# Layer 0 of the first batch item moved into the lanes, and the last bias among the mixtures

## Chip, cores and metric

One core of a Trainium2 chip. The metric is device time in microseconds, the median of several executions: 484.26 us for the kernel before (three executions, 484.23 to 484.34). All data are float32.

## What is computed

x has 32 batch items of 128 channels by 2048 positions. Four conditional residual layers follow each other:

```
x = x + W_a(n) x + b_a(n)                 # layer 0: 128x128 matrix of item n
x = x + conv(x, 9 taps, 4 groups) + ctx(n) + bias      # layer 1
x = x + W_2(n) x + b_2(n)                 # layer 2
x = x + W_3(n) x + b_3(n)                 # layer 3
W_l(n) = sum_k att_l(n, k) * weight_l[k]   # a mixture of 8 matrices
att_l  = softmax(gelu(gelu(cond W0 + b0) W1 + b1) W2 + b2)
```

## The kernel before, in words

The preparation computes the attention shares of all 32 items, the mixtures a0 (layer 0, identity added), a2 and a3, and for each item the product of a2 and a3, called m, so that layers 2 and 3 are one matrix. The biases of the layers are folded into c0 (added behind layer 0), d (behind the convolution) and e (at the end); e is itself a sum of matmuls over a2's bias, a3's weights w3 and a3's own bias.

PSUM has eight banks of 512 columns: four in cv_ps and four in aux_ps. Positions are split into four phases of 512. Three pieces run for each item: layer 0 (`layer0_steps`, L488, into aux_ps), the convolution (`conv_steps`, L508, into cv_ps) and the output product (`out_steps`, L537, into aux_ps). Every operand is split into a high part (fp32r) and a rest (hi and lo), and three matmuls stand for one. Each matmul uses 32 rows of the array; four generators, the lanes (`lane`, L544), one for each quarter of the rows, are advanced in turn by `in_turn` (L561), so that four matmuls on four row groups make a round. A lane starts 2 rounds behind the lane before it (LAG). In rounds, layer 0 and the output product have 12 each and the convolution 36. ScalarE copies each PSUM bank out as the high part (x1_hi, x2_hi), VectorE subtracts it from the bank to get the rest (x1_lo, x2_lo).

Order of PE's work in the preparation (L567 to L589): the hidden layers, the attention transposes with the matmul of bias d between them, 12 rounds of mixtures (`mixtures`, L431, also four row groups in turn; 24 banks in a ring of seven), the small biases, 8 more rounds, bias_e options 0 to 3 (L464, L466; L466 uses all 128 rows), the mixtures' remaining rounds, bias_e options 4 to 7, pair groups 0 to 3 (`quad_product`, L444, four products each, 128 rows, a ring of the four cv_ps banks), layer 0 of item 0 into aux_ps, pair groups 4 to 7, and then the lanes, which begin with layer 0 of item 1. Mixture banks are copied out by ScalarE (L600) and VectorE (L746) in a fixed share; the m banks by ScalarE (L641).

a0 makes a round trip through DRAM, so that each row group gets its own copy: SP saves the first pair, waits, issues four replicas (L286), then loads x of item 1 (L275), saves the other pairs, and so on, in one queue. GpSimd splits a0_rep into a0_hi and a0_lo (L696, L698), for item 0 behind the conversion of the convolution's weights (L722 to L726).

Of the kernel before, what the change touches and what calls it, by code (L numbers as in the profile page):

```python
# [13 lines left out]
B = 32  # L14
L = 2048
K = 8
# [18 lines left out]
DMA = 16  # L35
PAIR = 2
QUAD = 4
REPEAT = 4
HALVES = 2
PER = PH // HALVES  # L40
# [20 lines left out]
def wait(eng, semaphore, value):  # L61

    if value > 0:
        eng.wait_ge(semaphore, value)


def cond_resid_kernel(nc, x, net, consts, mix, bias, conv, c_weight, w3, out):
    with ExitStack() as ctx:
# [184 lines left out]
            return mix_out_a if BY_SCALAR[t] else mix_out_v, sum(by == BY_SCALAR[t] for by in BY_SCALAR[:t + 1])  # L253


        h_ps = [[cv_ps[:, h, 0:REPEAT * B]] + [aux_ps[:, 2 * h + n, 0:REPEAT * B] for n in range(NL - 1)] for h in range(2)]
        logits_ps = cv_ps[:, 2, 0:K]
        att_ps = aux_ps[:, 0, 0:NB].rearrange("p (n b) -> p n b", b=B)
# [8 lines left out]
        def _(sp):  # L267
# [9 lines left out]
            def save(src, scratch, first, last, saved):  # L277

                sp.dma_start(scratch[first:last].rearrange("q p x -> p q x"),
                             src[:, PAIR * first:PAIR * last, :].rearrange("p (q n) m -> p q (n m)",  # L280
                                                                           n=PAIR)).then_inc(saved, DMA)
# [7 lines left out]
            def replicate_a0(pair, phases):  # L289
                if pair < B // PAIR:  # L290
                    sp.wait_ge(a0_saved[min(pair, 1)], DMA)
                    wait(sp, a0_split, 2 * PAIR * (pair - 1))
                    replicate(a0_dram, a0_rep, a0_rep_loaded, pair, phases)
# [31 lines left out]
            load_half(0, 0)  # L325
            load_half(0, 1)
            sp.dma_start(w3_sb, w3.rearrange("p (k m) -> p k m", k=K)).then_inc(e_loaded, DMA)
            sp.dma_start(conv_f[:], conv).then_inc(conv_loaded, DMA)
            sp.wait_ge(d_ready, 1)
            sp.dma_start(d_dram, d_sb[:]).then_inc(d_saved, DMA)  # L330

            sp.wait_ge(*mix_taken(NOG - 2))
            sp.wait_ge(*mix_taken(NOG - 1))
            save(a0_all, a0_dram, 0, 1, a0_saved[0])
            replicate_a0(0, range(PH))
            load(1)
            save(a0_all, a0_dram, 1, B // PAIR, a0_saved[1])
# [33 lines left out]
        def _(pe):  # L371
# [23 lines left out]
            def attention():  # L395


                pe.wait_ge(consts_loaded, DMA)
                pe.wait_ge(shares_ready, 1)
                pe.matmul(att_ps.rearrange("p n b -> p (n b)"), shares[:].rearrange("q c k o -> q (c k o)"),  # L400
                          eye_sb[0:NB, 0:NB], start=True, stop=True).then_inc(att_made, 1)
                bias_d()
                pe.matmul(att_t_ps.rearrange("k n b -> k (n b)"), shares[:, 0, :, 0], eye_sb[0:NB, 0:NB], start=True,
                          stop=True).then_inc(att_t_made, 1)

# [6 lines left out]
            def bias_d():  # L412
                pe.wait_ge(c_weight_loaded, DMA)
                pe.matmul(d_ps, cw_sb[:], cond_sb, start=True, stop=True)
# [41 lines left out]
                          start=True, stop=True)  # L456
                pe.matmul(c2_ps, bias_sb[:, 1, :], att_t[:, 1, :], start=True, stop=True).then_inc(c_made, 1)

            def bias_e(options):
                if 0 in options:  # L460
                    pe.wait_ge(e_loaded, DMA)
                    pe.wait_ge(c2_att_ready, 1)
                    for n in range(1, NL):
                        pe.matmul(e_ps, bias_sb[:, n, :], att_t[:, n, :], start=(n == 1), stop=False)  # L464
                for k in options:
                    mm = pe.matmul(e_ps, w3_sb[:, k, :], c2_att[:, k, :], start=False, stop=(k == K - 1))  # L466
                return mm

            def layer0_steps(n, p):

                if n == 0 and p == 0:

                    pe.wait_ge(e_out, 1)
                pe.wait_ge(a0_split, 2 * (n + 1))

                wait(pe, y_out, PH * (n - 3) + p + 1)
                if n in (1, 2):
                    pe.wait_ge(x1_lo_done, PH * (n - 1) + p + 1)  # L480
                i, steps = 0, 3 * G
                for g in range(G):
                    h = g // PER
                    if g % PER == 0:
                        pe.wait_ge(x_lo_done, HALVES * n + h + 1)
                    hi, lo = x_parts(n, h)
                    for w, a in ((a0_hi, hi), (a0_lo, hi), (a0_hi, lo)):
                        mm = pe.matmul(aux_ps[:, p, :], w[n % 2][rows(p), g, :], a[rows(p), g % PER, :],  # L488
                                       start=(i == 0), stop=(i == steps - 1))
                        i += 1  # L490
                        if i == steps:
                            mm.then_inc(l0_done, 1)
                        yield

            def conv_steps(n, g):

                if n == 0 and g == 0:
                    pe.wait_ge(conv_split, 2)
                    pe.wait_ge(zero_cols, 4)
                    pe.wait_ge(m_out, B // QUAD)  # L500
                if g == 0:
                    pe.wait_ge(x1_lo_done, PH * (n + 1))
                wait(pe, x2_lo_done, PH * (n - 1) + g + 1)
                i, steps = 0, 3 * TAPMATS
                for j in range(TAPMATS):
                    s, q = j // PH, j % PH
                    for w, a in ((conv_hi, x1_hi), (conv_lo, x1_hi), (conv_hi, x1_lo)):
                        mm = pe.matmul(cv_ps[:, g, :], w[rows(g), j, :], a[n % 2][rows(g), q, s:s + T],  # L508
                                       start=(i == 0), stop=(i == steps - 1))
                        i += 1  # L510
                        if i == steps:
                            mm.then_inc(conv_done, 1)
                        yield
# [30 lines left out]
            def lane(g):  # L544

                for _ in range(LAG * g):
                    yield
                for n in range(B - 1):
                    yield from layer0_steps(n + 1, g)
                    conv = conv_steps(n, g)  # L550
                    if 0 < n < B - 2:
                        yield from itertools.islice(conv, CONV_A)
                        yield from out_steps(n - 1, g)
                    yield from conv

                yield from out_steps(B - 3, g)
                yield from conv_steps(B - 1, g)
                yield from out_steps(B - 2, g)
                yield from out_steps(B - 1, g)
# [12 lines left out]
                hidden(1, n)  # L572
            logits()
            fill(8)
            attention()
            mixing = [mixtures(c) for c in range(LANES)]

            in_turn(mixing, 3 * G)
            biases()
            in_turn(mixing, 2 * G)  # L580
            bias_e(range(0, 4))
            in_turn(mixing)
            bias_e(range(4, K)).then_inc(e_made, 1)
            for m in range(4):
                quad_product(m)
            in_turn([layer0_steps(0, p) for p in range(PH)])
            for m in range(4, B // QUAD):
                quad_product(m)
            in_turn([lane(g) for g in range(G)])  # L589

# [1 line left out]
        def _(act):  # L592
# [22 lines left out]
            def x1_out(n, phases=range(PH)):  # L615
                for p in phases:
                    act.wait_ge(l0_done, PH * n + p + 1)
                    nc.scalar.activation(x1_hi[n % 2][:, p, 1:T + 1], aux_ps[:, p, :], ACT.Identity,  # L618
                                         bias=c0_all[:, n:n + 1]).then_inc(x1_hi_done, 1)

            def x2_out(n):
# [22 lines left out]
            for t in range(MIXES):  # L644
                if BY_SCALAR[t]:
                    mix_evacuate(t)
            for m in range(3):
                m_evacuate(m)
            split_second_x_hi(0)
            m_evacuate(3)  # L650
            split_second_x_hi(1)
            act.wait_ge(bias_out, 1)
            x1_out(0)
            for m in range(4, B // QUAD):
                m_evacuate(m)
            for n in range(B):
                if 0 < n:
                    x2_out(n - 1)
# [12 lines left out]
        def _(pool):  # L671
# [47 lines left out]
            for q in range(PH):  # L719

                centre = conv_f[:, PH + q, rows(q)]
                nc.gpsimd.tensor_tensor(centre, centre, eye32_sb, ALU.add).then_inc(pool_chain, 1)  # L722
            pool.wait_ge(pool_chain, PH)
            nc.gpsimd.tensor_copy(conv_hi[:], conv_f[:]).then_inc(conv_split, 1)
            pool.wait_ge(conv_split, 1)
            nc.gpsimd.tensor_tensor(conv_lo[:], conv_f[:], conv_hi[:].bitcast(F32), ALU.subtract).then_inc(conv_split, 1)  # L726
            split_a0(0)
            split_a0(1)
            for n in range(B):
                if n + 2 < B:  # L730
# [4 lines left out]
        def _(dve):  # L735
# [31 lines left out]
            def x1_out(n):  # L767
                for p in range(PH):
                    dve.wait_ge(x1_hi_done, PH * n + p + 1)
                    nc.vector.scalar_tensor_tensor(x1_lo[n % 2][:, p, 1:T + 1], aux_ps[:, p, :], c0_all[:, n:n + 1],  # L770
                                                   x1_hi[n % 2][:, p, 1:T + 1].bitcast(F32), ALU.add,
                                                   ALU.subtract).then_inc(x1_lo_done, 1)

# [140 lines left out]
```

## Time and profile before

| | us |
|---|---|
| median of 3 executions | 484.26 |
| profiled execution | 484.1 |
| its span | 482.3 |
| busy in the span: PE, VectorE, ScalarE, GpSimd | 473.2, 320.2, 248.5, 151.2 |

The span is what the profile sees; the execution's own time has 1.8 us around it. Times of instructions are counted from the span's start. PE matmuls overlap, so the sum of single durations is far above the busy time.

### The profile page before, as it was taken

To read this page: it belongs to the slowest core of one execution; us is meant where nothing else is said; L and a number is where in the kernel's file an instruction comes from. 1 tells how busy PE (TensorE), PEld (TensorE's weight loads), DVE (VectorE), ACT (ScalarE), POOL (GpSimd) and SP (SyncE) were. 2 spreads that over 40 slices of the span, in tenths; PEclk is the share of its full clock that TensorE was granted. 3 is DMA by queue.
4 is the path that set the end of the run, shared out by engine and by line. 5 is a ranking of instruction groups with operands and counts; after the bars stand their busy time and mean duration, and the time that the engine had idled before them with its cause. 6 is when DMAs were issued, how large, how long until landed. Compare 5 with 4: busy or idle time off the path is not lost.

```text
span 482.3 us, 17714 instructions
## 1 busy us (share of the span) xinstructions
PE 473.2 (98%) x8003; PEld 446.3 (93%) x8003; DVE 320.2 (66%) x409; ACT 248.5 (52%) x414; POOL 151.2 (31%) x151
## 2 busy tenths in 40 slices
PE   8989999999999999999999999999999999999996
PEld 7978999999999999999999999999999999999995
DVE  3548687767676876767687776767777676777424
ACT  5654445466544545654455466444545654455544
POOL 2935072324133322414331331333223142420110
PEclk9999999999999999999999999999999999999998
DMA  8696977676546476664746666464667746452224
GB/s 277 207 334 184 302 232 226 209 221 208 186 120 215 156 217 219 207 216 112 211 149 217 209 214 216 129 206 140 215 203 220 220 149 208 131 187 77 90 88 175
DMA packets 39244, 92.86 MB, mean 193 GB/s; under 512 B 4601, under 2 KB 25473, under 8 KB 35201
## 3 DMA queue, kind: packets, MB, share of 16 engines
q1 hardware_dynamic: 39168, 91.73, 60.5%
q8 instruction: 63, 1.03, 0.9%
q14 instruction: 13, 0.10, 0.1%
HBM read 53.95 MB, written 37.77 MB: 190 GB/s over the span
## 4 chain that ended last, share of the span: by engine, by line
PE 97%; DMA 1%; issue 1%; DVE 0%; SPq 0%; DVEq 0%
PE cv_ps L508 59%; PE aux_ps L488 18%; PE aux_ps L537 15%; PE cv_ps L444 2%; PE cv_ps L431 1%; DMA consts_sb<-in_consts_dram 1%; PE cv_ps L537 1%; PE aux_ps L431 1%; PE aux_ps L466 0%; DVE y_all L847 0%; DVE m_all L797 0%; PE aux_ps L455 0%; PE aux_ps L400 0%; SPq L318 0%; SPq L319 0%
## 5 line engine op out<-in xcount | busy, mean ns | idle before, releaser
L508 PE MATMUL cv_ps<-x_hi,conv_lo 32*128 32x512 f32 x1536 | 284.7, 391 | 0.0
L508 PE MATMUL cv_ps<-x_hi,conv_hi 32*128 32x512 f32 x1536 | 284.2, 389 | 0.0
L508 PE MATMUL cv_ps<-x_lo,conv_hi 32*128 32x512 f32 x1536 | 284.2, 391 | 0.0
L508 PEld LDWEIGHTS cv_ps<-x_lo,conv_hi 32*128 32x128 f32 x1536 | 172.5, 184 | 4.7
L508 PEld LDWEIGHTS cv_ps<-x_hi,conv_hi 32*128 32x128 f32 x1536 | 171.5, 183 | 5.6
L508 PEld LDWEIGHTS cv_ps<-x_hi,conv_lo 32*128 32x128 f32 x1536 | 172.4, 183 | 4.5
L779 DVE SCALAR_TENSOR_TENSOR x_lo<-cv_ps,d_all,x_hi 128x512 fp32r<-128x512 f32 x128 | 87.2, 744 | 132.4 <-ACT x_hi L626 132.4
L636 ACT ACTIVATE y_all<-aux_ps,e_all 128x512 f32<-128x512 f32 x122 | 74.0, 689 | 134.1 <-PE aux_ps L537 134.1
L626 ACT ACTIVATE x_hi<-cv_ps,d_all 128x512 fp32r<-128x512 f32 x128 | 77.5, 688 | 67.9 <-PE cv_ps L508 67.9
L488 PE MATMUL aux_ps<-x_hi,a_hi 32*128 32x512 f32 x512 | 99.5, 391 | 2.3 <-issue 2.3
L488 PE MATMUL aux_ps<-x_hi,a_lo 32*128 32x512 f32 x512 | 99.1, 388 | 0.0
L488 PE MATMUL aux_ps<-x_lo,a_hi 32*128 32x512 f32 x512 | 99.0, 388 | 0.0
L537 PE MATMUL aux_ps<-x_hi,m_hi 32*128 32x512 f32 x496 | 94.8, 387 | 0.0
L537 PE MATMUL aux_ps<-x_hi,m_lo 32*128 32x512 f32 x496 | 94.3, 387 | 0.0
L753 DVE TENSOR_TENSOR x_lo<-x_sb,x_hi 128x1024 fp32r<-128x1024 f32 x62 | 86.8, 1401 | 10.3 <-ACT x_hi L612 8.2
L537 PE MATMUL aux_ps<-x_lo,m_hi 32*128 32x512 f32 x496 | 93.5, 384 | 0.0
L770 DVE SCALAR_TENSOR_TENSOR x_lo<-aux_ps,c_all,x_hi 128x512 fp32r<-128x512 f32 x128 | 87.3, 745 | 1.6
L696 POOL CAST a_hi<-a_rep 128x512 fp32r<-128x512 f32 x32 | 26.6, 830 | 189.2 <-DMA a_rep<-a_pairs 124.7
L618 ACT ACTIVATE x_hi<-aux_ps,c_all 128x512 fp32r<-128x512 f32 x128 | 77.5, 691 | 12.9 <-PE aux_ps L488 12.9
L488 PEld LDWEIGHTS aux_ps<-x_hi,a_hi 32*128 32x128 f32 x512 | 58.8, 183 | 4.5 <-issue 2.4
L488 PEld LDWEIGHTS aux_ps<-x_lo,a_hi 32*128 32x128 f32 x512 | 58.5, 183 | 2.1
L488 PEld LDWEIGHTS aux_ps<-x_hi,a_lo 32*128 32x128 f32 x512 | 58.6, 184 | 1.7
(104 smaller groups left out, 455.5 us busy)
## 6 DMA issues: line engine op xcount, KB each, us to landing
x_sb<-in_x_dram SPq DMA_DIRECT2D x31, 1024.0 KB, 6.5
out_dram<-y_all SPq DMA_DIRECT2D x60, 512.0 KB, 7.4
a_rep<-a_pairs SPq DMA_DIRECT2D x64, 128.0 KB, 7.3
m_rep<-m_pairs SPq DMA_DIRECT2D x64, 128.0 KB, 6.1
out_dram<-y_all SPq DMA_DIRECT2D x8, 256.0 KB, 2.6
a_pairs<-a_all SPq DMA_DIRECT2D x1, 1920.0 KB, 12.4
m_pairs<-m_all SPq DMA_DIRECT2D x1, 1792.0 KB, 12.2
m_all<-in_mix_dram SPq DMA_DIRECT2D x2, 512.0 KB, 5.5
```

The costliest lines, as they stand in the source:

```text
L431: mm = pe.matmul(mix_ps[t % MIX_RING][:, P * j:P * (j + 1)], mix_f[layer][rows(c), G * h + j, :], spread[rows(c), layer].rearrange("p b o ...
L444: mm = pe.matmul(prep_ps[m % RING][:, P * k:P * (k + 1)], a23_all[0][:, n, :], a23_all[1][:, n, :], start=True, stop=True)
L488: mm = pe.matmul(aux_ps[:, p, :], w[n % 2][rows(p), g, :], a[rows(p), g % PER, :], start=(i == 0), stop=(i == steps - 1))
L508: mm = pe.matmul(cv_ps[:, g, :], w[rows(g), j, :], a[n % 2][rows(g), q, s:s + T], start=(i == 0), stop=(i == steps - 1))
L537: mm = pe.matmul(out_bank(n, p), w[n % 2][rows(p), g, :], a[n % 2][rows(p), g, :], start=(i == 0), stop=(i == steps - 1))
L618: nc.scalar.activation(x1_hi[n % 2][:, p, 1:T + 1], aux_ps[:, p, :], ACT.Identity, bias=c0_all[:, n:n + 1]).then_inc(x1_hi_done, 1)
L626: nc.scalar.activation(x2_hi[n % 2][:, g, :], cv_ps[:, g, :], ACT.Identity, bias=d_all[:, g, n:n + 1]).then_inc(x2_hi_done, 1)
L636: nc.scalar.activation(y_all[:, k % YBUFS, p % PER, :], bank[:, p, :], ACT.Identity, bias=e_all[:, n:n + 1]).then_inc(y_out, 1)
L696: nc.gpsimd.tensor_copy(a0_hi[n % 2][:], src).then_inc(a0_split, 1)
L753: nc.vector.tensor_tensor(lo, x_sb[n % 2][:, PER * h:PER * (h + 1)], hi.bitcast(F32), ALU.subtract).then_inc(x_lo_done, 1)
L770: nc.vector.scalar_tensor_tensor(x1_lo[n % 2][:, p, 1:T + 1], aux_ps[:, p, :], c0_all[:, n:n + 1], x1_hi[n % 2][:, p, 1:T + 1].bitcast(F32 ...
L779: nc.vector.scalar_tensor_tensor(x2_lo[n % 2][:, g, :], cv_ps[:, g, :], d_all[:, g, n:n + 1], x2_hi[n % 2][:, g, :].bitcast(F32), ALU.add, ...
```

## The change

Five edits. (1) `bias_d` is issued ahead of `attention`, so ahead of its wait for the shares. (2) `bias_e` becomes a generator that is advanced with the mixtures: behind the small biases it lets four rounds pass and then issues one step a round, two of L464 and eight of L466. (3) All eight pair groups are issued in one row behind the mixtures. (4) Layer 0 of item 0 is the first piece of the lanes and writes into the banks of cv_ps (`l0_bank`); phase p waits until the pair group that last used its bank is copied out. The wait for e_out moves to item 1, and ScalarE copies all eight groups ahead of item 0's x1, with the two halves of item 1's x_hi behind groups 3 and 5. (5) The DMA that loads the convolution's weights is issued behind the save of the first a0 pair, and GpSimd splits item 0's a0 ahead of converting these weights.

```diff
+        def l0_bank(n, p):
+            return prep_ps[p] if n == 0 else aux_ps[:, p, :]
...
-            sp.dma_start(conv_f[:], conv).then_inc(conv_loaded, DMA)
             sp.wait_ge(d_ready, 1)
...
             save(a0_all, a0_dram, 0, 1, a0_saved[0])
+            sp.dma_start(conv_f[:], conv).then_inc(conv_loaded, DMA)
             replicate_a0(0, range(PH))
...
-                bias_d()
...
+            def bias_e():
+                for _ in range(E_BEHIND):
+                    yield
+                pe.wait_ge(e_loaded, DMA)
+                pe.wait_ge(c2_att_ready, 1)
+                for n in range(1, NL):
+                    pe.matmul(e_ps, bias_sb[:, n, :], att_t[:, n, :], start=(n == 1), stop=False)
+                    yield
+                for k in range(K):
                     mm = pe.matmul(e_ps, w3_sb[:, k, :], c2_att[:, k, :], start=False, stop=(k == K - 1))
+                    if k == K - 1:
+                        mm.then_inc(e_made, 1)
+                    yield
...
             def layer0_steps(n, p):
-                if n == 0 and p == 0:
-                    pe.wait_ge(e_out, 1)
                 pe.wait_ge(a0_split, 2 * (n + 1))
-                wait(pe, y_out, PH * (n - 3) + p + 1)
-                if n in (1, 2):
-                    pe.wait_ge(x1_lo_done, PH * (n - 1) + p + 1)
+                if n == 0:
+                    pe.wait_ge(m_out, RING + p + 1)
+                elif n == 1:
+                    if p == 0:
+                        pe.wait_ge(e_out, 1)
+                elif n == 2:
+                    pe.wait_ge(x1_lo_done, PH + p + 1)
+                else:
+                    pe.wait_ge(y_out, PH * (n - 3) + p + 1)
...
+                yield from layer0_steps(0, g)
                 for n in range(B - 1):
...
             fill(8)
+            bias_d()
             attention()
...
-            in_turn(mixing, 2 * G)
-            bias_e(range(0, 4))
-            in_turn(mixing)
-            bias_e(range(4, K)).then_inc(e_made, 1)
-            for m in range(4):
-                quad_product(m)
-            in_turn([layer0_steps(0, p) for p in range(PH)])
-            for m in range(4, B // QUAD):
+            in_turn([*mixing, bias_e()])
+            for m in range(B // QUAD):
                 quad_product(m)
...
-            for m in range(3):
+            for m in range(B // QUAD):
                 m_evacuate(m)
-            split_second_x_hi(0)
-            m_evacuate(3)
-            split_second_x_hi(1)
+                if m in (3, 5):
+                    split_second_x_hi(m // 5)
             act.wait_ge(bias_out, 1)
             x1_out(0)
-            for m in range(4, B // QUAD):
-                m_evacuate(m)
...
+            split_a0(0)
             pool.wait_ge(pool_chain, PH)
...
-            split_a0(0)
             split_a0(1)
```

## Rows read from the trace of the kernel before

**Rows 1.** Page, PE's busy time, share of the span, instructions

```profile
PE 473.2 (98%) x8003; PEld 446.3 (93%) x8003; DVE 320.2 (66%) x409; ACT 248.5 (52%) x414; POOL 151.2 (31%) x151
```

**Rows 2.** Chain that ended last: start us, us, what

```profile
19.23 1.01 PE aux_ps L466 x8
20.26 3.84 PE cv_ps L444 x32
24.10 2.26 issue
26.36 3.48 PE aux_ps L488 x44
29.84 3.77 PE cv_ps L444 x32
...
62.79 3.28 PE cv_ps L508 x54
...
76.72 3.27 PE cv_ps L508 x55
```

**Rows 3.** Timeline of GpSimd: start us, us, instruction, count, idle before

```profile
18.48 0.83 POOL L722 TENSOR_TENSOR conv_f<-conv_f,consts_sb 128x32 f32<-128x32 f32 x4
19.38 1.46 POOL L724 CAST conv_hi<-conv_f 128x1536 fp32r<-128x1536 f32 x1
...
24.30 0.61 POOL L696 CAST a_hi<-a_rep 128x512 fp32r<-128x512 f32 x1
24.99 1.26 POOL L698 TENSOR_TENSOR a_lo<-a_rep,a_hi 128x512 fp32r<-128x512 f32 x1
```

**Rows 4.** Timeline of PE: bias d, first matmuls of the lanes

```profile
8.71 0.33 PE L414 MATMUL aux_ps<-m_rep,cw_sb 128*128 128x32 f32 x2
...
33.54 0.51 PE L488 MATMUL aux_ps<-x_hi,a_hi 32*128 32x512 f32 x2
```

**Rows 5.** Timeline of ScalarE

```profile
18.14 1.08 ACT L600 ACTIVATE m_all<-aux_ps 128x512 f32<-128x512 f32 x2 [1.52 <-PE aux_ps L431]
19.11 1.09 ACT L600 ACTIVATE m_all<-cv_ps 128x512 f32<-128x512 f32 x2
...
27.35 1.06 ACT L612 ACTIVATE x_hi<-x_sb 128x1024 fp32r<-128x1024 f32 x1 [3.51 <-DMA x_sb<-in_x_dram]
...
36.59 2.42 ACT L618 ACTIVATE x_hi<-aux_ps,c_all 128x512 fp32r<-128x512 f32 x4 [2.34 <-PE aux_ps L488]
45.02 2.42 ACT L626 ACTIVATE x_hi<-cv_ps,d_all 128x512 fp32r<-128x512 f32 x4 [6.00 <-PE cv_ps L508]
```

**Rows 6.** Timeline of VectorE

```profile
19.26 0.69 DVE L746 COPY m_all<-cv_ps 128x512 f32<-128x512 f32 x1 [0.19 <-PE cv_ps L431]
...
45.81 2.73 DVE L779 SCALAR_TENSOR_TENSOR x_lo<-cv_ps,d_all,x_hi 128x512 fp32r<-128x512 f32 x4 [0.86 <-ACT x_hi L626]
```

**Rows 7.** Timeline of SP's queue: start and length of the issue

```profile
17.90 2.61 SPq L286 DMA_DIRECT2D a_rep<-a_pairs  x4
20.56 0.44 SPq L275 DMA_DIRECT2D x_sb<-in_x_dram  x1
```

**Rows 8.** Page, DMA issues: count, KB, us from issue to landing

```profile
a_pairs<-a_all SPq DMA_DIRECT2D x1, 128.0 KB, 4.4
```

**Rows 9.** Timeline of PE where mixtures and the last bias meet

```profile
14.60 0.34 PE L431 MATMUL cv_ps<-spread,a_rep 32*128 32x128 f32 x1
...
15.12 0.36 PE L431 MATMUL cv_ps<-spread,a_rep 32*128 32x128 f32 x2
...
15.81 0.38 PE L464 MATMUL aux_ps<-att_t,bias_sb 8*128 8x32 f32 x2
16.12 1.08 PE L466 MATMUL aux_ps<-c_att,m_rep 128*128 128x32 f32 x8
17.13 0.37 PE L431 MATMUL aux_ps<-spread,a_rep 32*128 32x128 f32 x1
...
17.35 0.27 PE L431 MATMUL cv_ps<-spread,a_rep 32*128 32x128 f32 x1
```

More of the change, by code:

```diff
@@ L37 @@
 QUAD = 4
+E_BEHIND = 4
 REPEAT = 4
@@ L457, in biases @@
                 pe.matmul(c2_ps, bias_sb[:, 1, :], att_t[:, 1, :], start=True, stop=True).then_inc(c_made, 1)
[L459 to L465, printed above, removed]
+            def bias_e():
[7 more added lines that the diff above has]
+                for k in range(K):
                     mm = pe.matmul(e_ps, w3_sb[:, k, :], c2_att[:, k, :], start=False, stop=(k == K - 1))
-                return mm
+                    if k == K - 1:
+                        mm.then_inc(e_made, 1)
+                    yield
             def layer0_steps(n, p):
-                if n == 0 and p == 0:
-                    pe.wait_ge(e_out, 1)
                 pe.wait_ge(a0_split, 2 * (n + 1))
-                wait(pe, y_out, PH * (n - 3) + p + 1)
-                if n in (1, 2):
-                    pe.wait_ge(x1_lo_done, PH * (n - 1) + p + 1)
+                if n == 0:
[7 more added lines that the diff above has]
+                    pe.wait_ge(y_out, PH * (n - 3) + p + 1)
                 i, steps = 0, 3 * G
@@ L487, in layer0_steps @@
                     for w, a in ((a0_hi, hi), (a0_lo, hi), (a0_hi, lo)):
-                        mm = pe.matmul(aux_ps[:, p, :], w[n % 2][rows(p), g, :], a[rows(p), g % PER, :],
+                        mm = pe.matmul(l0_bank(n, p), w[n % 2][rows(p), g, :], a[rows(p), g % PER, :],
                                        start=(i == 0), stop=(i == steps - 1))
@@ L499, in conv_steps @@
                     pe.wait_ge(zero_cols, 4)
-                    pe.wait_ge(m_out, B // QUAD)
                 if g == 0:
@@ L617, in x1_out @@
                     act.wait_ge(l0_done, PH * n + p + 1)
-                    nc.scalar.activation(x1_hi[n % 2][:, p, 1:T + 1], aux_ps[:, p, :], ACT.Identity,
+                    nc.scalar.activation(x1_hi[n % 2][:, p, 1:T + 1], l0_bank(n, p), ACT.Identity,
                                          bias=c0_all[:, n:n + 1]).then_inc(x1_hi_done, 1)
@@ L769, in x1_out @@
                     dve.wait_ge(x1_hi_done, PH * n + p + 1)
-                    nc.vector.scalar_tensor_tensor(x1_lo[n % 2][:, p, 1:T + 1], aux_ps[:, p, :], c0_all[:, n:n + 1],
+                    nc.vector.scalar_tensor_tensor(x1_lo[n % 2][:, p, 1:T + 1], l0_bank(n, p), c0_all[:, n:n + 1],
                                                    x1_hi[n % 2][:, p, 1:T + 1].bitcast(F32), ALU.add,
```

## The prediction

> **What bounds the kernel now.** I began with the page's first lines: PE is busy 98% of the span [rows 1]. Then the chain of waits in order of time [rows 2]: nearly all of it is PE, and in steady state an item repeats every 76.72 - 62.79 = 13.93 us. An item is 12 + 36 + 12 = 60 rounds of four row-tiled matmuls, so a round is 0.232 us. The chain names PE through the lanes without a break; the change leaves every one of those rounds in place, so it can act only ahead of and at the start of the lanes. There the chain has one hole, 2.26 us at 24.10, between the fourth pair group and layer 0 of item 0. The GpSimd timeline says what it is [rows 3]: a0_hi and a0_lo of item 0 come behind the conversions of conv and end at 26.25; PE resumes at 26.36.
>
> **What goes.** Before, from the first pair group (20.26) to the first lane matmul (33.54, [rows 2, 4]) 13.28 us pass: 3.84 for four groups, the 2.26, 3.41 for layer 0 of item 0 with its own slow start and end, 3.77 for the other four groups. After, the eight groups stand in one row, 3.84 + 3.77 = 7.61 us, and layer 0 of item 0 is 12 more rounds of the lanes, 12 x 0.232 = 2.79. The lag of six rounds is paid once in either kernel. 13.28 - 10.40 = 2.88 us go, if nothing is late.
>
> **What is late next.** Measure from S, the end of the pair groups.
> - The first convolution. Lane 0 reaches it 24 rounds after S, S + 5.57, and waits for x1_lo of all four phases. Lane 0's layer 0 is through at S + 2.79; ScalarE starts on such a bank 0.26 after it (36.59 against 33.54 + 2.79) [rows 4, 5]; VectorE starts 0.79 after ScalarE (45.81 against 45.02) and takes 2.73 for four [rows 5, 6]. Sum S + 6.57: a new wait of 1.0 us. Before, item 0's x1 was made while PE ran groups 4 to 7, so nothing waited. Bounds: 0.7, if four x1_lo took only their pitch behind the last ScalarE one, and 1.3. I take 1.0.
> - The a0 splits. GpSimd now takes item 0's a0 ahead of the conversions of conv. From the arrival R of a0_rep: 1.95 for item 0, 5.0 for conv_hi and conv_lo, 1.95 for item 1, R + 9.0 [rows 3]. Layer 0 of item 1 wants it at S + 2.79. R is at most about 22.3 (the four replicas were issued at 17.90 to 20.51, [rows 7], and had arrived when GpSimd came to them at 24.30), which gives 31.3: in time for S above 28.5. The conv parts are wanted later still.
> - Groups 4 to 7 on ScalarE. It does m 0 to 3, x_hi(1,0), m 4, 5, x_hi(1,1), m 6, 7. Item 1's x landed at 27.35 [rows 5], issued at 20.56 behind the a0 round trip, whose save took 4.4 us [rows 7, 8]. With conv out of the queue ahead of that save it may come back up to 2 us sooner: arrival X between 25.4 and 27.4. From X, two splits of 0.96 and four copies of 0.55 each end at X + 4.2, and phase 3 wants the last of them at S + 1.4. That costs nothing if S is above X + 2.8, and up to 1.9 if S stays near 27.9 and X at 27.35.
>
> **The last bias among the mixtures.** This decides the sign. Before, its two shares stand in blocks: eight L466 matmuls in 1.08 us, a pitch of 0.11, twice [rows 9, 2]; the second block, from 19.23, hides the evacuation of the last mixture banks (ScalarE until 20.20, VectorE until 19.95 [rows 5, 6]), and the first group starts at 20.26. After, one step (two passes) of it stands in each of rounds 16 to 25 of the mixtures. The first two (L464, 8 rows) are row-tiled like the mixtures and cost about their pitch. The eight of L466 use all 128 rows. What the trace shows of going between the two: the last L464 starts at 16.19 - 0.27 = 15.92 and the first L466 at 16.12, 0.20 later; the last L466 starts at 17.20 - 0.28 = 16.92 and the first mixture matmul at 17.13, 0.21 later; that round's second pass then comes at 17.35, 0.22 later instead of 0.09 to 0.11 (15.12, two in 0.36) [rows 9]. So a mixture round with one L466 step in it is 0.21 + 0.02 (four lanes' starts) + 0.20 + 0.13 (the step's second pass, a little over the pitch of the block) + 0.21 = 0.77 us, where the mixture round is 0.22 (two passes) and the bias step in a block 0.22. Rounds 16 and 17 start at 14.60 [rows 9], less 0.14, because the d bias now stands ahead of the wait for the shares instead of between two matmuls behind it (two passes in 0.33, of which mixtures can win some 0.14; 0 to 0.26 [rows 4]). 14.46 + 2 x 0.45 = 15.36, + 8 x 0.77 = 21.52, + the last round's second pass and latency 0.21 + 0.27 = 22.0. Then nothing covers the last evacuation: 0.03 + 0.69 + 0.05 [rows 6]. The first group starts at 22.8, 2.5 later than before. Evacuation (one bank of 0.6 to 0.7 a round of 0.77, on two engines) does not bind there.
> Lower bound: switches overlap fully, a round with its step costs 0.22 + 0.22 = 0.44; 15.36 + 3.6 + 0.5 + 0.8 = 20.2, no change. Upper bound: another 0.1 for each of 16 switches, 24.4. I take 22.8, since it is made of the gaps that these very two kinds of matmul show.
>
> The page "TensorEngine Tiling (Array Packing)", section Key Properties, of the Trainium skill says that changing the tiling mode drains TensorE; the gaps of 0.20 and 0.21 agree, as no L466 starts until the tile matmuls before it are about over. Its page "TensorE: Matmul & The Clock Gate", section "Step-by-step: what each phase is for", says that weight loads are pulled ahead of running matmuls where row groups don't conflict or the spare weight buffer takes them. By that second rule alone the round would come to 0.44 and the sum to the lower bound; it stands as the first rival.
>
> **The sum.** -2.88 + 1.0 + 2.5 = +0.65 us; S is then 30.4, so neither the a0 splits (31.3 against 33.2) nor ScalarE (X + 2.8 at most 30.2) is late. Moving conv's load costs nothing by itself: it is issued about 13.9, behind the save, into a queue that before had passed all loads and the save by 17.90 [rows 7, 8]; GpSimd came to conv_f only at 18.48 [rows 3], and the converted weights are wanted at S + 6.6. The profiled execution took 484.1 (span 482.3 and 1.8 around it); the median is 484.26. 484.1 + 0.65 = 484.75, beside the median 484.9; I say 484.8. About 0.2% (0.97 us) is what a measurement of this kernel can tell from no change.
>
> **Rivals.**
> 1. Interleaved steps are nearly free (0.44 a round). First group at 20.2, S = 27.8. Then X counts: with X = 25.6 ScalarE is late by 0.4. -2.88 + 1.0 + 0.4 = -1.5: 482.7. For it: behind the first L466 block ScalarE waited 1.52 us on PE [rows 5], a wait that spreading the steps removes. Against it: the gaps. Chance 0.17.
> 2. Half of it: switches cost, but the slow second pass overlaps, and some of the steps fall into waits for banks. 0.6 a round, first group at 21.4. -2.88 + 1.0 + 1.2 = -0.7: 483.5. Chance 0.25.
> 3. On the other side: the a0 round trip gets late. The 768 KB of conv now go into the one queue between the save of the first a0 pair and its replicas. If the replicas come 3.5 us late, R is near 26, a0 of item 1 is ready at 35 against S + 2.79 = 33.2, and item 1's x is late by as much (X = 30, ScalarE 34.2 against 31.8). The larger of the two, 2.4 us, comes on top: +3.0, 487.2. It decides from R = 24.2 or X = 27.6. Against it: before, conv stood ahead of the save as well, and both were in by 17.90 [rows 7]. Chance 0.08.
> 4. The change doesn't do what it says, as the hole moves: the new wait is over 1.3 us, and each switch costs 0.05 more than its gap (0.8 in all, half of the upper bound's extra). -2.88 + 1.3 + 3.3 = +1.7: 485.9. Chance 0.12.
> My forecast (within 0.8 of +0.65) has 0.38.
>
> **The numbers.** Faster by over 0.2%: nearly all of rival 1, a third of rival 2: 0.24. Slower by over 0.2%: rivals 3 and 4 and a fifth of the forecast: 0.27. Within: 0.49. The range goes from rival 1 to rival 4, 482.6 to 486.0; the forecast's own is 484.0 to 485.6.
>
> **What would show it.** In PE's timeline L466 matmuls in pairs, 0.77 apart, from about 15.8 to 21.3; the first L444 at 22.8 (20.2 for rival 1); eight groups without a hole, 7.6 us; at once L488 into the convolution's banks; a gap of 1.0 ahead of the first L508, released by VectorE's x1_lo; no gap after it, and 13.93 us for each item. GpSimd's a0 before conv_hi. The forecast is wrong if the first group starts before 21.5, if a gap appears between groups or inside layer 0 of item 0, or if a later item is longer.

## The result, and the profile after

The changed kernel takes 489.85 us (median of 4 executions, 489.09 to 492.64) against 484.30 (median of 4, 484.23 to 485.70): ratio 1.0123, 95% interval 1.0092 to 1.0154. I had said 484.8 and at most 486.0. It is slower by 5.5 us, well outside the range. In this document an execution that is over 1.5% above the fastest of its kernel, at a lower clock, is left out of ratios, intervals and ranges of times.

The profiled execution took 490.46, its span is 488.7 (before: 482.3). Its chain of waits in order of time (start us, us, what), beside [rows 2]:

```profile
18.21 0.34 PE aux_ps L473 x2
...
18.98 0.34 PE aux_ps L473 x2
...
19.75 0.34 PE aux_ps L473 x2
...
20.61 0.57 PE aux_ps L473 x2
...
21.92 0.56 PE aux_ps L473 x2
...
23.22 0.56 PE aux_ps L473 x2
...
24.51 0.56 PE aux_ps L473 x2
...
26.67 9.23 PE cv_ps L448 x64
35.91 3.00 PE cv_ps L500 x36
...
38.98 0.70 ACT x_hi L625
...
39.78 1.72 DVE x_lo L774 x3
...
41.77 0.75 DVE x_lo L774
...
42.66 0.47 PE cv_ps L519
```

L473 is the old L466, L448 the pair groups, L500 layer 0, L519 the convolution. The first bias steps stand 0.77 us apart (18.21, 18.98, 19.75), as forecast; but from the fifth on they stand 1.30 apart, and the pair groups take 9.23 us instead of 7.61. The stretches of the profile after say why (length, busy time and count of PE, PE's weight loads, VectorE, ScalarE, GpSimd, then the granted TensorE clock, DMA share, GB/s):

```profile
10.00:15.00 5.00, 5.00 (x96) 4.94 (x97) 3.21 (x7) 2.88 (x5) 4.34 (x5) 0.66 0.63 243
20.00:25.00 5.00, 5.00 (x35) 3.85 (x34) 0.69 (x1) 2.05 (x4) 1.87 (x6) 0.53 0.94 248
25.00:30.00 5.00, 4.12 (x18) 3.85 (x18) 0.79 (x2) 0.74 (x2) 4.92 (x3) 0.50 1.07 387
30.00:35.00 5.00, 5.00 (x45) 5.00 (x44) 1.06 (x1) 3.83 (x7) 2.60 (x3) 0.94 0.89 314
```

The granted clock is at 0.5, its lower level of 1.2 GHz, from 20.3 to 30.6 us, and once before that, from 10.1 to 13.5. In the profile of before it stands at 1.00 in every such stretch from 5 to 40 us. PE counts as busy in these rounds (5.00 of 5.00 from 20 to 25 us), so how little it does in these rounds is read off the starts of its matmuls and off their count, 35 in 5 us.

GpSimd (timeline), beside [rows 3]: item 0's a0 now comes first, but a0_rep is there only at 23.89, and item 1's a0 is ready at 32.68.

```profile
20.91 0.83 POOL L726 TENSOR_TENSOR conv_f<-conv_f,consts_sb 128x32 f32<-128x32 f32 x4 [2.10 <-DMA conv_f<-in_conv_dram]
23.89 0.61 POOL L700 CAST a_hi<-a_rep 128x512 fp32r<-128x512 f32 x1 [2.15 <-DMA a_rep<-a_pairs]
24.57 1.26 POOL L702 TENSOR_TENSOR a_lo<-a_rep,a_hi 128x512 fp32r<-128x512 f32 x1
...
27.33 3.46 POOL L731 TENSOR_TENSOR conv_lo<-conv_f,conv_hi 128x1536 fp32r<-128x1536 f32 x1
30.71 0.62 POOL L700 CAST a_hi<-a_rep 128x512 fp32r<-128x512 f32 x1
31.41 1.27 POOL L702 TENSOR_TENSOR a_lo<-a_rep,a_hi 128x512 fp32r<-128x512 f32 x1
```

**Where the 6.4 us of the two spans are.** The first pair group starts 6.41 later (26.67 against 20.26 [rows 2]). Of that 1.5 are there at the small biases already (L454 started at 12.55, its successor at 14.03: the clock of 10.1 to 13.5, and a start 0.3 us later). Another 2.2 are what the lower clock costs from the fifth bias step on: the steps start 0.86, 1.31, 1.30 and 1.29 after each other, and the round behind the last one takes 1.30 (24.51 to 25.81), all five instead of 0.77. The 2.7 that remain are the price of the steps and of the last evacuation at the upper clock; the forecast has them at 2.7 as well, less 0.14 for the first edit. The groups cost 1.6 more. Then -2.88, and +1.2 for the wait ahead of the first convolution. 6.41 + 1.6 - 2.88 + 1.2 = 6.3, which is how much later the first convolution starts (42.66 against 36.39). From that convolution to PE's end it is 441.9 us, against 441.5 before: the lanes are nearly what they were. The executions at 489.1 and 489.2 have a mean granted clock of 0.989 against 0.985 in the profiled one, as they would without the first fall; but the one at 492.64 has 0.988, and none of them has a trace, so this isn't shown.

### The profile page after: what moved, and what is told of

The parts are those of the page before. It is cut to its first block, busy times and chain, and to the rows that moved or that the text cites. A ratio compares the mean times of both kernels' runs of the same rounds, so it can differ in the third digit from the quotient of the medians.

```text
span 488.7 us, 17713 instructions
## 1 busy us (share of the span) xinstructions
PE 480.3 (98%) x8003; PEld 421.5 (86%) x8003; DVE 320.0 (65%) x409; ACT 249.4 (51%) x414; POOL 153.9 (31%) x151
## 4 chain that ended last, share of the span: by engine, by line
PE 97%; DVE 1%; ACT 1%; DMA 0%; issue 0%; DVEq 0%; ACTq 0%
PE cv_ps L519 55%; PE aux_ps L548 18%; PE aux_ps L500 16%; PE cv_ps L448 2%; PE cv_ps L435 2%; PE cv_ps L548 1%; PE aux_ps L435 1%; PE aux_ps L473 1%; PE cv_ps L500 1%; DVE x_lo L774 1%; DMA m_rep<-in_net_dram 0%; PE aux_ps L390 0%; ACT L613 0%; PE cv_ps L390 0%; DVE y_all L851 0%
## 5 line engine op out<-in xcount | busy, mean ns | idle before, releaser
L519 PE MATMUL cv_ps<-x_hi,conv_hi 32*128 32x512 f32 x1536 | 326.2, 389 | 1.1 <-DVE x_lo L774 1.1
L519 PE MATMUL cv_ps<-x_hi,conv_lo 32*128 32x512 f32 x1536 | 326.6, 391 | 0.0
L519 PE MATMUL cv_ps<-x_lo,conv_hi 32*128 32x512 f32 x1536 | 326.3, 391 | 0.0
L519 PEld LDWEIGHTS cv_ps<-x_hi,conv_hi 32*128 32x128 f32 x1536 | 236.5, 183 | 13.4 <-issue 1.4
L519 PEld LDWEIGHTS cv_ps<-x_lo,conv_hi 32*128 32x128 f32 x1536 | 236.8, 184 | 13.0
L519 PEld LDWEIGHTS cv_ps<-x_hi,conv_lo 32*128 32x128 f32 x1536 | 236.7, 183 | 11.1
L500 PE MATMUL aux_ps<-x_lo,a_hi 32*128 32x512 f32 x496 | 115.4, 388 | 0.0
L500 PE MATMUL aux_ps<-x_hi,a_lo 32*128 32x512 f32 x496 | 115.1, 388 | 0.0
L500 PE MATMUL aux_ps<-x_hi,a_hi 32*128 32x512 f32 x496 | 114.9, 389 | 0.0
L757 DVE TENSOR_TENSOR x_lo<-x_sb,x_hi 128x1024 fp32r<-128x1024 f32 x62 | 84.4, 1362 | 10.1 <-ACT x_hi L619 8.0
L548 PEld LDWEIGHTS aux_ps<-x_hi,m_hi 32*128 32x128 f32 x496 | 81.4, 183 | 3.2
L548 PEld LDWEIGHTS aux_ps<-x_hi,m_lo 32*128 32x128 f32 x496 | 81.6, 183 | 2.6
L548 PEld LDWEIGHTS aux_ps<-x_lo,m_hi 32*128 32x128 f32 x496 | 81.7, 183 | 2.5
L500 PEld LDWEIGHTS aux_ps<-x_hi,a_lo 32*128 32x128 f32 x496 | 80.7, 184 | 3.1
```

What stands on the lines that cost most here:

```text
L500: mm = pe.matmul(l0_bank(n, p), w[n % 2][rows(p), g, :], a[rows(p), g % PER, :], start=(i == 0), stop=(i == steps - 1))
L548: mm = pe.matmul(out_bank(n, p), w[n % 2][rows(p), g, :], a[n % 2][rows(p), g, :], start=(i == 0), stop=(i == steps - 1))
L757: nc.vector.tensor_tensor(lo, x_sb[n % 2][:, PER * h:PER * (h + 1)], hi.bitcast(F32), ALU.subtract).then_inc(x_lo_done, 1)
```

## The experiments

Each is timed beside the kernel before, which had a median of 484.2 to 484.3 in all calls.

**1. Which part costs: four kernels.** The bias back in two blocks, all else as changed:

```diff
-            in_turn([*mixing, bias_e()])
+            in_turn(mixing, 2 * G)
+            last_bias = bias_e()
+            in_turn([last_bias], NL - 1 + 4)
+            in_turn(mixing)
+            in_turn([last_bias])
```

> The changed kernel with one edit undone: the last bias stands in two blocks again, as before the change. Theory A (the interleaved 128-row steps cost 0.77 us a round, and their gaps bring TensorE's clock down to the lower level until the pair groups are over): the first pair group starts near 20.2 us, the clock stays at its upper level from there, the span loses the 2.88 us and pays about 1.2 for the wait ahead of the first convolution: 482.5 to 483.0 us. Theory B (eight pair groups in a row, or layer 0 in the lanes, bring the clock down, wherever the bias stands): the groups still take 9.2 us or more, 485 to 487 us.

Measured: 486.74 us, 1.0039 (1.0025 to 1.0053). The groups take 7.41, so theory B is out; but it isn't 482.5 to 483.0 either. Its chain of waits has left PE:

```profile
23.92 0.62 POOL a_hi L704
...
24.61 1.27 POOL a_lo L706
25.88 1.42 POOL conv_hi L733
...
27.37 3.46 POOL conv_lo L735
30.82 1.56 POOL a_hi L704
...
32.46 2.14 POOL a_lo L706
...
34.64 0.64 PE aux_ps L500
```

Layer 0 of item 1 waits 1.89 us for its a0, ready at 34.6, and right behind that hole the clock is at its lower level from 34.8 to 38.2. The changed kernel hid this, since its groups end at 35.9. Splitting item 1's a0 took 3.8 us here instead of 1.9, while VectorE was splitting item 1's x out of SBUF:

```profile
27.82 5.64 DVE L761 TENSOR_TENSOR x_lo<-x_sb,x_hi 128x1024 fp32r<-128x1024 f32 x2 [5.26 <-ACT x_hi L623]
```

That slowdown is the whole hole: with 1.95 for the split, a0 would have been ready at 30.78 + 1.95 = 32.73 (an estimate), and PE was through with item 0 at 32.75. Part of the rest of the miss is the clock at the start, which rose only at 14.4 in this profile.

The bias step alone, on the kernel before (`bias_e` made a generator as in the change):

```diff
-            in_turn(mixing, 2 * G)
-            bias_e(range(0, 4))
-            in_turn(mixing)
-            bias_e(range(4, K)).then_inc(e_made, 1)
+            in_turn([*mixing, bias_e()])
```

> The kernel before with only the last bias interleaved with the mixtures. Theory A: the first pair group starts 22.7 to 26, the hole ahead of layer 0 of item 0 closes (a0 is ready at 26.25), and the clock falls during the interleaved rounds as in the changed kernel: 487 to 489 us, nearly the whole loss. Theory B: the drain alone, +2.5 less the hole of 2.26: 484.5 to 485 us, clock at its upper level.

Measured: 489.17 us, 1.0097 (1.0077 to 1.0116). One edit has nearly the whole loss; the first group starts at 25.10, and the clock is low from 18.8 to 29.0, again from the fifth bias step on (19.04).

The fifth edit alone, on the kernel before:

```diff
-            sp.dma_start(conv_f[:], conv).then_inc(conv_loaded, DMA)
...
             save(a0_all, a0_dram, 0, 1, a0_saved[0])
+            sp.dma_start(conv_f[:], conv).then_inc(conv_loaded, DMA)
...
+            split_a0(0)
             pool.wait_ge(pool_chain, PH)
...
-            split_a0(0)
             split_a0(1)
```

> The kernel before with only the fifth edit: conv's load behind the save of the first a0 pair, and item 0's a0 split ahead of conv's conversions. Both theories: a0 of item 0 is ready near 24.3 instead of 26.25 and the hole of 2.26 us shrinks to 0.2 to 0.5; 482.3 to 482.8 us. If the replicas come later behind conv's 768 KB (rival 3 of the prediction) the hole stays: 484 us.

Measured: 485.14 us, 1.0014 (1.0004 to 1.0023): a small loss, not a gain. The hole ahead of item 0 did shrink, to 0.19 us at 24.14; a new one of 1.48 us opened at 31.55 ahead of item 1, whose a0 came behind conv's conversions, and again the clock was low for 3.4 us behind it (34.1 to 37.5). I had looked at the first hole only.

```profile
33.03 0.70 PE L488 MATMUL aux_ps<-x_hi,a_hi 32*128 32x512 f32 x2 [1.49 <-POOL a_lo L698]
```

The split of this a0 took 3.8 us here too (29.16 to 32.98), beside VectorE's split of x; with 1.95 it would have been ready at 31.1 (an estimate), ahead of the 31.54 at which PE wanted it.

The eight L466 steps cut to 8 rows, which leaves most of the last bias's sum out; nothing else is changed:

```diff
-   mm = pe.matmul(e_ps, w3_sb[:, k, :], c2_att[:, k, :], start=False, stop=(k == K - 1))
+   mm = pe.matmul(e_ps, w3_sb[0:K, k, :], c2_att[0:K, k, :], start=False, stop=(k == K - 1))
```

> The changed kernel with the eight L466 steps cut to 8 rows, so that they are row-tiled like the mixtures (this leaves most of the last bias's sum out). Same number of instructions in the same places. Theory A (it is the change of tiling and its gaps): rounds of 0.35 to 0.45 us instead of 0.77, the first group near 20.3, clock at the upper level: 482.5 to 483.3 us. Rival (it is the number of instructions among the mixtures, or their semaphores): rounds stay near 0.77 and the time stays at 489 us.

Measured: 486.34 us, 1.0032 (1.0018 to 1.0046). The steps stand 0.45 us apart, with the same number of instructions, and the clock stays up among them:

```profile
20.65 0.03 PE aux_ps L473
...
21.09 0.03 PE aux_ps L473
...
21.54 0.03 PE aux_ps L473
```

So the price of a round is that of going from row-tiled to 128-row matmuls and back. The forecast of 482.5 to 483.3 was missed all the same. In the profile the clock is low from 9.4 to 19.6, just ahead of these steps, and PE waits 1.07 us for the last mixture banks, which ScalarE copies until 24.05; the first group starts at 24.10, not near 20.3. Item 1's a0 is ready at 34.0 there, just ahead of its use at about 34.3; that an execution with an earlier start has to wait for it isn't shown.

**2. Why the clock falls, and what a switch costs.** Three matmuls on zeros behind each step (they take one bank out of the mixtures' ring, which has six then instead of seven):

```diff
                     mm = pe.matmul(e_ps, w3_sb[:, k, :], c2_att[:, k, :], start=False, stop=(k == K - 1))
+                    for _ in range(FILLERS):
+                        pe.matmul(aux_ps[:, 0, 0:2 * P], idle_sb[:, 0:P], idle_sb[:], start=True, stop=True)
```

> The changed kernel with three matmuls of 256 columns on zeros behind each L466 step (24 in all, into a PSUM bank taken out of the mixtures' ring, which has six banks instead of seven). Theory A (TensorE's clock falls because the interleaved rounds leave it idle between the switches): with more work in each gap-ridden round the clock stays at its upper level; a round costs 0.77 + 0.35, the first group starts near 25.7, the groups take 7.6 again: 487 to 488 us, less than the 489.85 of the changed kernel although there is more to do. Rival (the clock falls at that point whatever PE does): the fillers cost twice as much, 491 to 493 us.

Measured: 492.14 us, 1.0134 (1.0108 to 1.0160). The time falls in the rival's range and above my 487 to 488, the trace goes against the rival: the clock never falls among the bias steps or the groups. The fillers (L476) come every 1.20 to 1.21 us from the first round to the last, where the changed kernel went from 0.77 to 1.30:

```profile
20.03 0.44 PE aux_ps L476 x3
21.24 0.43 PE aux_ps L476 x3
...
26.06 0.43 PE aux_ps L476 x3
27.26 0.43 PE aux_ps L476 x3
28.46 0.43 PE aux_ps L476 x3
```

The stretches have the granted clock at 1.00, where the changed kernel had 0.53 and 0.50:

```profile
20.00:25.00 5.00, 5.00 (x55) 3.98 (x55) 1.58 (x3) 1.19 (x2) 1.36 (x5) 1.00 0.94 264
25.00:30.00 5.00, 4.30 (x38) 3.21 (x36) 0.94 (x3) 1.79 (x3) 4.84 (x4) 1.00 1.01 353
```

The mean granted clock is 0.999 in the three executions that count, against 0.985 to 0.989 for the changed kernel. The fillers cost 0.43 a round, not 0.35, and the clock rose only at 14.9 in the profile, so the first group starts at 30.18 instead of 25.7; what the smaller ring adds to that was not tested. So with more work in the rounds the clock holds, whatever the time since the start; but bought with idle work it isn't worth its price.

Two bias steps a round in four rounds, on the kernel before with the bias interleaved (marked against the kernel of one step a round):

```diff
-                    yield
+                    if k % 2:
+                        yield
```

> The kernel before with the last bias among the mixtures, but two L466 steps a round in four rounds: 8 switches of tiling instead of 16, the same matmuls. Theory A (each switch has a price): four rounds of 0.99 and the rest of 0.22, first group near 21.3 if the clock holds: 484.3 to 485.5 us against 489.17 with one step a round; PE's share is higher in such a round, so the clock should hold longer. Rival (the price is in the interleaving as such): 488 to 489 us.

Measured: 487.15 us, 1.0058 (1.0032 to 1.0083), between the kernel before and the one with one step a round, above my 484.3 to 485.5, and wide: 483.9 to 490.1. In the profiled one (492.61) the clock was low from 9.2 to 33.1, so its rounds can't be held against 0.99; but at that same low clock a round with two steps took 1.73 us (22.302 to 24.035) where the changed kernel's round with one took 1.30. The second step adds 0.43 and the way there and back is paid once. Five of the other eleven executions kept a mean granted clock of 0.993 or more, which none of the fifteen did that the three kernels with one step a round have between them (the changed one, the bias step alone, and the one interleaved again in part 3: 0.985 to 0.991). With half the switches the clock falls for less time, in some executions.

**3. The other edits.** The third and fourth alone, on the kernel before (the parts of the change's diff in `layer0_steps`, `lane`, the row of groups and ScalarE's order):

> The kernel before with only the third and fourth edit: all pair groups in one row, layer 0 of item 0 first in the lanes, in the convolution's banks. Item 1's x then comes at 27.35 as before. Theory: -2.88, +1.2 for the wait ahead of the first convolution, and ScalarE's last m copy at 27.35 + 4.2 = 31.5 against 29.3, +2.2: 484.8 us, with PE's holes inside layer 0 of item 0. Rival (the order of the groups pays on its own): 482.5 to 483 us.

Measured: 484.47 us, 1.0009 (0.9995 to 1.0024). The number is right; the mechanism was not seen. In the profile the clock was low from 9.0 to 19.3, so the groups ended at 31.3 and ScalarE was in time. Whether holes inside layer 0 of item 0 stand behind the faster executions (483.6 and up) stays open.

Then a version without both losses: bias in blocks, conv's load put behind item 1's x, both first a0 splits ahead of conv:

```diff
             save(a0_all, a0_dram, 0, 1, a0_saved[0])
-            sp.dma_start(conv_f[:], conv).then_inc(conv_loaded, DMA)
             replicate_a0(0, range(PH))
             load(1)
+            sp.dma_start(conv_f[:], conv).then_inc(conv_loaded, DMA)
...
+            split_a0(0)
+            split_a0(1)
             pool.wait_ge(conv_loaded, DMA)
...
-            split_a0(0)
...
-            split_a0(1)
```

> The changed kernel with the bias in two blocks, conv's load put behind item 1's x, and GpSimd converting conv behind both first a0 splits. Theory C (in the kernel with the blocks the time is lost where a0 of item 1 waits for conv's conversions on GpSimd, ready at 34.6): a0 of item 1 is ready by 24 to 26 us, no wait ahead of layer 0 of item 1, only 1.2 us ahead of the first convolution, no fall of the clock there: 482.3 to 482.9 us. Rival (the lanes' start itself is slow): as with the blocks, 485 to 487 us.

Measured: 483.28 us, 0.9982 (0.9962 to 1.0001), not to be told from the kernel before and above my 482.3 to 482.9. Both first a0 are ready by 26.8. No hole but the 1.04 us ahead of the first convolution. The executions spread from 481.9 to 484.4, with two at 486: in the profiled one the clock rose only at 14.1.

The same kernel with the bias interleaved again:

> The best kernel so far (bias in blocks, conv's load behind item 1's x, both first a0 splits ahead of conv's conversions: 483.28 us) with one edit: the last bias interleaved again, one step a round. Theory A (drains 2.5 us, and the clock falls in these rounds until the groups are over, 3 to 4 us more): 487 to 490 us, clock at the lower level from about 19 or 20 us on, rounds of 0.77 turning to 1.29. Rival (in the changed kernel it was the late a0 of item 1 behind conv that cost most, and the interleaving only 2.5): 485 to 486 us.

Measured: 489.28 us, 1.0106 (1.0089 to 1.0123). With no late a0 the one edit costs 6 us, with the clock low from 20.4 to 30.6, here from behind the sixth step:

```profile
19.26 0.34 PE aux_ps L473 x2
...
20.03 0.34 PE aux_ps L473 x2
...
21.10 0.56 PE aux_ps L473 x2
...
22.39 0.56 PE aux_ps L473 x2
...
24.55 10.26 PE cv_ps L448 x64
34.81 2.99 PE cv_ps L500 x39
```

More filling at the start (`fill(12)` for `fill(8)`), and bias d between the transposes again:

> The best kernel so far with 12 instead of 8 filling matmuls ahead of the attention. Theory D (the spread of its runs, 481.9 to 486.6, is the clock at the start: it falls again near 9 to 10 us or rises only at 14, and nothing downstream absorbs that shift any more): a denser start makes the late rise or the fall rarer, median 482.3 to 482.8, though 0.2 to 0.9 us are lost where the clock is low while it fills. Rival (these matmuls don't decide it): same median, 483.3, same spread.

> The best kernel so far with the first edit undone: the matmul of bias d between the two attention transposes again. Prediction's step: it is worth 0.14 us at most 0.26, so 483.3 to 483.5 us, not to be told from the best kernel. Rival (with the d bias ahead PE stands idle longer before the transposes, and the clock falls there): the spread shrinks and the median comes to 482.4.

Measured: 483.90 us (0.9986, 0.9969 to 1.0002) and 483.61 us (0.9979, 0.9969 to 0.9989). Neither can be told from the 483.28 of the version they start from. With more filling the mean granted clock was 0.998 or more in all eleven executions, but they still spread from 482.2 to 485.5, so theory D isn't shown. (This mean leaves out the time before the clock's first rise: in the profile of the version it starts from it is 0.999, although the clock rose only at 14.1.) The first edit is worth nothing that can be measured. The trace of the last shows the order that the forecast counted on, with an early clock:

```profile
20.14 7.41 PE cv_ps L449 x64
27.55 3.00 PE cv_ps L501 x36
...
30.63 0.70 ACT x_hi L629
...
31.43 1.72 DVE x_lo L778 x3
...
33.41 0.75 DVE x_lo L778
```

It also showed a wait of its own: layer 0 of item 2 for item 1's x1_lo. An edit that was to remove it:

```diff
             x1_out(0)
+            x1_out(1)
             split_x(2, 0)
...
-                if n + 1 < B:
+                if 0 < n < B - 1:
                     x1_out(n + 1)
```

> The kernel with the d bias between the transposes (483.61 us) with one more edit: VectorE makes x1_lo of item 1 ahead of splitting item 2's x. In that kernel's trace layer 0 of item 2 waits 42.6 to 43.1 for x1_lo of item 1 (VectorE from 42.24, behind the splits of item 2's x, which lands only at 37.11), about 0.8 us in all. Theory: the wait goes, PE's stretch from the first convolution to its end falls from 442.8 to 442.0 us, 482.8 to 483.2 us. Rival (the split of item 2's second half, now ending near 43, becomes the wait): 483.4 to 483.8.

Measured: 483.04 us, 0.9975 (0.9956 to 0.9994); from the first convolution to PE's end 441.85 us instead of 442.80. The number is as expected, but it doesn't show that the edit removed the wait: the profiled execution had a late clock (first rise at 14.4), and the version without this edit has 441.87 in its own profile, with its rise at 14.1. The wait was seen only with an early clock. Against the kernel before (484.20 beside it) this version is 1.2 us faster, with an interval that ends just under 1; the four versions of this part without the interleaving (483.04 to 483.90) can't be told from each other. All are well ahead of the changed kernel.

## Why the prediction was wrong

- **The hole and the restarts, -2.88: right.** 7.41 us for the eight groups and layer 0 at once behind them, wherever the clock was up.
- **The wait ahead of the first convolution, 1.0: right.** 1.05 us idle, 1.2 by the starts (S to L519 is 6.75 in the profile after; 6.57 was forecast).
- **A bias step among the mixtures, 0.77 a round: right** to the hundredth where the clock is up, made of gaps read off four places in the trace of before. Rivals 1 and 2 were wrong. The gaps weighed more than what rival 1 goes by, which would have given 0.44.
- **The step that failed is the sum of the last bias at "8 x 0.77", and of the groups at 7.61: both took the upper clock for granted.** The sum itself has two gaps of 0.2 us in each round, and I never asked what the clock does then; the profile of before showed it at its upper level throughout. From the fifth step on a round took 1.30, and the groups 9.23: 2.2 + 1.6 = +3.8 us. The same fall came in each profiled kernel that had one step a round (20.3, 18.8 and 20.4 us), after four, four and six steps, and none came in that place with row-tiled steps or with fillers. That it is the idle time between the switches that brings the clock down is what the fillers speak for; no run separates it from the switches as such. The page "TensorE: Matmul & The Clock Gate" of the Trainium skill has a case like it, section "A second HAM failure mode: psum-queue depth-cycling": in another kernel, short idle stretches between groups of matmuls made the clock swing. I had read that page for weight loads only; the runs agree with this section.
- **The shift of the start, no term at all.** Before, the first group could start up to 2.3 us later at no cost, since layer 0 waited for a0 until 26.36 anyway [rows 2]. With the hole closed, a late rise or an early fall of the clock at the start goes straight into the time (1.5 us in the profile after).
- **The fifth edit "costs nothing": wrong, though hidden in the changed kernel.** I took R to be at most 22.3, which the rows don't give: they only bound it by GpSimd's start at 24.30. R was 23.9 in the profile after and item 1's a0 ready at 32.7, which is in time for the forecast's S of 30.4 (33.2) too. What failed is the term of 1.95 for item 1's split: beside VectorE's split of x it took 3.8, in the two traces where PE then waited for it. By itself the edit loses 0.9 us. Rival 3 had the place right and gave it 0.08, but for another reason, late replicas; with the fifth edit alone they were in at 22.27 and PE waited all the same.
- **A slip that changes nothing.** Rival 1 has ScalarE late by 0.4 with X = 25.6 and S = 27.8; X + 2.8 is 28.4, so it is 0.6.

## What to carry to other kernels

Where 128-row and row-tiled matmuls alternate, price each crossing from a gap in the trace, and keep each kind in a block. Then ask what the idle time so made does to the clock: until it rises again work that wasn't touched is slower too (here the groups, 9.23 us instead of 7.61). And when a hole is closed, the delays that it had absorbed come due; look at the next wait on the same engine before counting the hole as gain.

## What the runs showed of the hardware

- TensorE's granted clock fell among rounds with two gaps of 0.2 us in 0.77, and not among rounds of 1.21 us that held three matmuls of 256 columns more.
- A single wait of 1.5 to 1.9 us at 31 to 33 us (the fifth edit alone, the bias in blocks) was followed by 3.4 us at the lower level; the hole of 2.26 us of before was not, nor the wait of 1.05 us ahead of the first convolution.
- The same start gives different clocks: in the traces the first rise comes at 4.8 to 6.8 us (ten of them) or at 14.1 to 14.9 (four), and kernels with the same instructions up to there are found in both groups (the changed kernel 6.7, the blocks 14.4). In the version with conv's load last a mixture matmul takes 0.42 us up to 13.5 and 0.27 from 14.2.
- GpSimd split item 1's a0 in 3.8 us while VectorE subtracted two SBUF operands (5.64 us for two that otherwise take 1.22 each), against 1.9 alone. In the trace of the blocks they take turns: conv_lo keeps its 3.46 us and ends at 30.82, VectorE's first subtraction, begun at 27.82, ends 1.09 later; a_hi, begun at 30.78, ends 0.47 after that (32.38); VectorE's second ends at 33.46, and a_lo, begun at 32.46, ends 1.13 later (34.59). With the fifth edit alone the same waits come out at 1.08, 0.47 and 1.13. The Trainium skill, "SBUF — State Buffer", section "Who interferes with whom", has a VectorE instruction with two SBUF inputs and a GpSimd one that reads SBUF contend for a shared port pair that one locks for a whole instruction; these turns agree.
